# Attention stage: the value products of two units issued together every second unit, with three buffers of exponentials and two slots of part rows

## The reference

```python
# first attention: rotary embedding on q and k, no mask
att = softmax(einsum('bhqd,bhkd->bhqk', q, k) / sqrt(16));  y = att @ v;  x = x + y @ wo.T
# second attention: no rotary embedding, a linear bias by distance and a causal mask
att = softmax(q @ k / sqrt(16) + alibi + causal_mask);      y = att @ v;  x = x + y @ W_o
```

## Time and profile before

| what | value |
|---|---|
| median of three runs | 2952.81 us |
| the profiled execution's own time | 2950.72 us |
| its span in the trace | 2948.9 us |
| TensorE busy | 2667.6 us, 90% |
| VectorE busy | 1946.6 us, 66% |
| ScalarE busy | 1261.4 us, 43% |
| GpSimd busy | 657.1 us, 22% |
| granted TensorE clock, mean | 0.949 |

### The profile page before, as it was taken

How to read it: one execution, slowest core, us unless ns; L and a number is a source line. 1 busy time by engine, 2 the same in 40 slices (tenths; PEclk the granted TensorE clock), 3 DMA queues, 4 the chain that set the end, 5 groups by cost and what they waited for, 6 DMA issues and landing times. The chain is left out here.

```text
span 2948.9 us, 40309 instructions
## 1 busy us (share of the span) xinstructions
PE 2667.6 (90%) x14292; PEld 1275.0 (43%) x14292; DVE 1946.6 (66%) x4227; ACT 1261.4 (43%) x1901; POOL 657.1 (22%) x640
## 2 busy tenths in 40 slices
PE   3987999999999999797999995999999999798997
PEld 2442233333333332354455663454544454455564
DVE  5877878777877885585774334767677674576333
ACT  1432456556655667443211221355455556221221
POOL 0554122131230300153002441222121100001341
PEclk8996899999999999998999997799999999899998
DMA  3004330321303300001202663633233430301566
GB/s 118 1 1 101 49 60 12 54 50 22 60 17 49 58 8 1 1 1 61 92 33 49 137 135 85 129 64 57 45 61 54 66 50 2 107 33 33 122 138 166
DMA packets 163075, 175.78 MB, mean 60 GB/s; under 512 B 19570, under 2 KB 136242, under 8 KB 162738
## 3 DMA queue, kind: packets, MB, share of 16 engines
q1 hardware_dynamic: 145348, 150.48, 22.9%
q0 software_dynamic: 12416, 17.84, 3.8%
q10 hardware_dynamic: 5120, 4.98, 0.5%
HBM read 116.32 MB, written 56.13 MB: 58 GB/s over the span
## 5 line engine op out<-in xcount | busy, mean ns | idle before, releaser
L1776 DVE TENSOR_REDUCE a_mx<-a_bank 128x1 f32<-128x512 f32 (+3 forms) x1792 | 1031.0, 627 | 285.3 <-PE a_bank L1517 219.0
L1653 ACT ACTIVATE a_E<-a_bank 128x1024 f32<-128x1024 f32 (+3 forms) x896 | 794.8, 932 | 477.5 <-PE a_bank L1574 328.3
L1517 PE MATMUL a_bank<-a_KT,a_QT 96*128 96x512 bf16 (+4 forms) x1792 | 597.0, 379 | 35.1 <-DVE a_mx L1776 25.2
L1574 PE MATMUL a_bank<-a_QT,a_KT 99*128 99x512 bf16 (+4 forms) x1792 | 510.7, 360 | 18.5 <-DMA a_QT<-a_mT 16.0
L1589 PE MATMUL a_bank<-a_E,a_Vg 128*32 128x512 f32 (+3 forms) x3584 | 442.3, 566 | 0.7 <-ACT a_E L1653 0.7
L1517 PEld LDWEIGHTS a_bank<-a_KT,a_QT 96*128 96x128 bf16 (+1 forms) x1792 | 152.2, 98 | 526.1 <-DVE a_mx L1776 305.6
L1574 PEld LDWEIGHTS a_bank<-a_QT,a_KT 99*128 99x128 bf16 (+1 forms) x1792 | 170.4, 99 | 199.0 <-ACT a_E L1653 37.0
L848 PE MATMUL d_bank<-wdT,d_hT 128*128 128x256 f32 (+1 forms) x768 | 201.9, 407 | 21.7 <-DVE x L1054 21.7
L960 ACT ACTIVATE d_silu<-d_bank 128x512 f32<-128x512 f32 x96 | 57.2, 596 | 375.6 <-PE d_bank L835 368.4
L1044 DVE SCALAR_TENSOR_TENSOR d_silu<-d_silu,d_bank 128x512 f32<-128x512 f32 x96 | 65.6, 683 | 227.3 <-ACT d_silu L960 219.9
L433 POOL TENSOR_TENSOR f_hl<-f_hT,f_hh 128x512 f16<-128x512 f32 x96 | 111.1, 1157 | 392.1 <-ACT f_hh L452 392.1
(11 more groups left out here) (234 smaller groups left out, 3537.8 us busy)
## 6 DMA issues: line engine op xcount, KB each, us to landing
parts<-a_parts SPq DMA_DIRECT2D x64, 384.0 KB, 2.5
a_QT<-parts SPq DMA_DIRECT2D x180, 128.0 KB, 5.4
a_KT<-parts SPq DMA_DIRECT2D x180, 128.0 KB, 8.0
d_wgu<-in_L_ffn_w_gate SPq DMA_DIRECT2D x64, 176.0 KB
d_wgu<-in_L_ffn_w_up SPq DMA_DIRECT2D x64, 176.0 KB
d_wd<-in_L_ffn_w_down SPq DMA_DIRECT2D x64, 176.0 KB
normalised<-d_xn SPq DMA_DIRECT2D x8, 1152.0 KB, 4.7
acc<-d_zero SPq DMA_DIRECT2D x66, 128.0 KB, 1.8
```

The lines of the kernel that those rows point to most:

```text
L1517: last = nc.tensor.matmul(out[:, 0:w], QT[0:W, h, qt * P:(qt + 1) * P], KT[0:W, h, kh * HALF:kh * HALF + w], start=True, stop=not diag)
L1574: last = nc.tensor.matmul(out, KT[:, h, kt * P:(kt + 1) * P], QT[:, h, half * HALF + c0:(half + 1) * HALF], start=True, stop=not diag)
L1653: nc.scalar.activation(E[:, u % 2, 2 * pair:2 * pair + 2, c0:HALF], bank[:, 2 * pair:2 * pair + 2, c0:HALF], ACT.Exp).then_inc(exps, 1)
L1776: nc.vector.tensor_reduce(mx[:, j, qt, kh:kh + 1], out[:, 0:w], AX.X, ALU.max).then_inc(freed_dve, 1)
```

## The change

- The value products are issued in even units only: in an even unit `u` those of `u-2` and then `u-1`, in unit 0 the last two of the group before. Odd units have none. After the last group the last two are issued as before.
- `E` has three buffers, used by `(G * U + u) % 3`; the exponentials of a unit wait for the products of the unit three before it.
- `Ysb` has one slot in place of two; a second copy waits for the `turn_y` of the first.
- `parts` has two slots in place of four. At the first sequence rows 2 and 3 are held in the third buffer of `E`, and the exponentials of group 0, unit 2 wait for their writes. `split` now waits for the write of two before (four before in the first cases).

```diff
-        parts = sb(tag + "parts", [P, 4, 3, HALF], BF16)
+        parts = sb(tag + "parts", [P, 2, 3, HALF], BF16)
-        E = sb(tag + "E", [P, 2, GH, HALF])
-        Ysb = sb(tag + "Ysb", [P, 2, HALF])
+        E = sb(tag + "E", [P, 3, GH, HALF])
+        Ysb = sb(tag + "Ysb", [P, HALF])
...
+        def part_rows(b, n):
+
+            if b == 0 and n in (2, 3):
+                rows = E[:, 2].rearrange("p j c -> p (j c)").bitcast(BF16)
+                return rows[:, (n - 2) * 3 * HALF:(n - 1) * 3 * HALF].rearrange("p (s c) -> p s c", s=3)
+            return parts[:, n % 2]
...
-                    if b or n >= 4:
-                        pool.wait_ge(written[n % 4], START + (done // 4) * 16)
+                    user = done - 2 if done >= 6 else done - 4
+                    pool.wait_ge(written[user % 4], START + (user // 4 + 1) * 16)
...
-                        if u:
+                        if u % 2 == 0 and u:
+                            pv_unit(G, u - 2)
                             pv_unit(G, u - 1)
-                        elif G:
+                        elif u % 2 == 0 and G:
+                            pv_unit(G - 1, U - 2)
                             pv_unit(G - 1, U - 1)
                         for x in beside[G, u][2:]:
                             fill(x)
+                pv_unit(BG - 1, U - 2)
                 pv_unit(BG - 1, U - 1)
...
-                    if pair == 0 and (G or u > 1):
-                        act.wait_ge(pv, START + G * U + u - 1)
+                    if pair == 0 and G * U + u > 2:
+                        act.wait_ge(pv, START + G * U + u - 2)
+                    if G == 0 and u == 2 and pair == 0:
+                        for n in (2, 3):
+                            act.wait_ge(written[n], START + 16)
...
-                    if G:
-                        act.wait_ge(filled, START + place["turn_y", G - 1, half] + 1)
-                    nc.scalar.activation(Ysb[:, half, :], bank[:, 4, :], ACT.Copy).then_inc(y_kept, 1)
+                    if G or half:
+                        act.wait_ge(filled, START + place["turn_y", G if half else G - 1, 1 - half] + 1)
+                    nc.scalar.activation(Ysb[:], bank[:, 4, :], ACT.Copy).then_inc(y_kept, 1)
```

More of the change, by code:

```diff
@@ L1395, in write @@
                     dst = dram["parts"][b, 1 - c % 2, :, c // 2 * P:(c // 2 + 1) * P, half * HALF:(half + 1) * HALF]
-                    sp.dma_start(dst.rearrange("s p t -> p s t"), parts[:, n % 4]).then_inc(written[n % 4], 16)
+                    sp.dma_start(dst.rearrange("s p t -> p s t"), part_rows(b, n)).then_inc(written[n % 4], 16)
                 def load(b, g):
@@ L1447, in split @@
                     at_ = slice(half * HALF, (half + 1) * HALF)
-                    p = parts[:, n % 4]
+                    p = part_rows(b, n)
                     if second:
@@ L1527, in fill @@
                         for i in range(KPH):
-                            last = nc.tensor.transpose(out[:, i * P:(i + 1) * P], Ysb[:, x[2], i * P:(i + 1) * P], ident)
+                            last = nc.tensor.transpose(out[:, i * P:(i + 1) * P], Ysb[:, i * P:(i + 1) * P], ident)
                     elif kind == "tokens":
@@ L1589, in pv_unit @@
                         last = nc.tensor.matmul(bank[VW * j:VW * (j + 1), 4, c0:HALF], Vg[:, G % NG, kt, VS * j:VS * j + VW],
-                                                E[:, u % 2, j, c0:HALF], start=first, stop=final, tile_position=(0, VW * j))
+                                                E[:, (G * U + u) % 3, j, c0:HALF], start=first, stop=final, tile_position=(0, VW * j))
                     last.then_inc(pv, 1)
@@ L1652, in exp_pair @@
                     act.wait_ge(scored, START + G * 2 * U + 2 * u + pair + 1)
-                    nc.scalar.activation(E[:, u % 2, 2 * pair:2 * pair + 2, c0:HALF], bank[:, 2 * pair:2 * pair + 2, c0:HALF],
+                    nc.scalar.activation(E[:, (G * U + u) % 3, 2 * pair:2 * pair + 2, c0:HALF], bank[:, 2 * pair:2 * pair + 2, c0:HALF],
                                          ACT.Exp).then_inc(exps, 1)
@@ L1668, in cast @@
                         act.wait_ge(roped_dve, START + 2 * n + 2)
-                    nc.scalar.activation(parts[:, n, 0], staged(0, n)[0], ACT.Copy).then_inc(high, 1)
+                    nc.scalar.activation(part_rows(0, n)[:, 0], staged(0, n)[0], ACT.Copy).then_inc(high, 1)
                 def cast_rest(n):
                     act.wait_ge(rest, START + n + 1)
-                    nc.scalar.activation(parts[:, n, 1], staged(0, n)[0], ACT.Copy).then_inc(mid, 1)
+                    nc.scalar.activation(part_rows(0, n)[:, 1], staged(0, n)[0], ACT.Copy).then_inc(mid, 1)
                 for x in ahead_of_rows[0:8]:
@@ L1744, in middle @@
                     dve.wait_ge(high, START + n + 1)
-                    nc.vector.tensor_tensor(staged(0, n)[0], staged(0, n)[0], parts[:, n, 0], ALU.subtract).then_inc(rest, 1)
+                    nc.vector.tensor_tensor(staged(0, n)[0], staged(0, n)[0], part_rows(0, n)[:, 0], ALU.subtract).then_inc(rest, 1)
                 def lower(n):
                     dve.wait_ge(mid, START + n + 1)
-                    nc.vector.tensor_tensor(parts[:, n, 2], staged(0, n)[0], parts[:, n, 1], ALU.subtract).then_inc(parted_dve, 1)
+                    nc.vector.tensor_tensor(part_rows(0, n)[:, 2], staged(0, n)[0], part_rows(0, n)[:, 1], ALU.subtract).then_inc(parted_dve, 1)
                 def maxima(G):
```

## The result

The changed kernel takes 2983.56 us (median of four runs, 2978.78 to 2988.76) against 2954.39 before (median of four): ratio 1.0096, 95% interval 1.0069 to 1.0123. It is slower, as forecast; the forecast of 2990, 1.0126 of the 2952.81 it was worked out from, lies just above the interval and above all four runs. The profiled execution spans 2977.7 us, 28.8 more than before.

A forecast was written before the change was run, and what follows sets the result against it. TensorE ends last, with VectorE close behind at 89% in plain first-stage groups. 29 + 6 + 0 + 2 = +37 on 2950.7 gives 2988, and 2.1 for the runs' median 2990 us; 8 in 10 from 2944 to 3012.

The forecast's parts named there:

- The block: Two units' value products together take 2.21 us; on TensorE alone a two-unit cycle falls from 5.67 to 5.47.
- the switch isn't saved: Rival: the second unit's weight loads wait, block 2.42 us, 45 us more than forecast, 3035 us; chance 0.04.
- VectorE rushed, the wait at h: Plain first-stage cycle: TensorE waits 0.38 us for a bank at h, its last odd-unit chunk; cycle 5.89 against 5.67.
- TensorE's gain comes through: Rival: VectorE keeps ahead of the three banks, each cycle gains 0.20 us, -45 in all, 2908 us; chance 0.08.
- ScalarE "isn't late": First-stage cycle: the odd unit's exponentials are there at 3.1 us, when TensorE comes at 3.25.
- The first stage's 29 us in chunk cycles: First-stage cycles with chunks lose 4 + 23 + 2 = 29 us over the groups; bounds -24 and +42.
- stalls are taken in: Rival: long items, DMA waits and clock dips absorb stalls, only last groups lose; 2950 to 2965 us; chance 0.12.
- Cycles without chunks: Ten first-stage cycles: ScalarE runs out of scores during the block, 5.0 to 5.1 us each for 4.23; +6 us.
- The second stage at 0: Its 88 chunk cycles gain 0.20 us and lose 0.19 each; put at 0, between -18 and +19.
- Values after the wait for `m_rows`: `turn_m` stands ahead of one more unit's products, one more lies behind the wait; the sum is the same, costing nothing.
- Buffers and narrow slots at nothing: Third `E` buffer, single `Ysb` and two `parts` slots cost nothing; late writes at the second stage's start are hidden.
- the narrow slots reach the path: Rival: at the second stage's start the two `parts` slots cost 10 us more, 3000 us; chance 0.04.

The follow-up runs named there:

- e5: The changed kernel with first-stage maxima over half the columns and first-stage exponentials over half the queries (from the fourth unit on); 2895.71 us.
- e6: The kernel before the change with first-stage maxima over half the columns and first-stage exponentials over half the queries; 2902.14 us.
- e3: The changed kernel with first-stage maxima taken over the first half of each chunk's columns only; 2921.58 us.
- e1: The changed kernel's buffers with the value products issued in every unit again; 2952.21 us against 2952.28 before, ratio 1.0001.
- e7: The changed kernel, but with products single wherever the unit of the block holds no chunk; 2979.05 us, ratio 1.0093 to the kernel before.
- e12: The kernel before with turn_m and the maxima rows' DMAs one unit earlier, and products together in the second stage only; 2937.15 us, ratio 0.9953.
- e8: The changed kernel with products together only in second-stage units 0 and 6 of a group (not the last group), all others single; 2959.28 us, ratio 1.0026.
- e4: The kernel before the change with first-stage maxima over half of each chunk's columns; 2904.56 us.
- e9: The changed kernel with three of an even unit's items ahead of the block in place of two; 2966.64 us, ratio 1.0051 to the kernel before.

## Why the prediction was right

- **The block.** Forecast 2.21 us, measured 2.16, and the gain on TensorE alone 0.20 against the 0.24 that e5 and e6 show. The switch is saved, so the rival "the switch isn't saved" (2.42) is out. The third stream came at the lower bound (0.43), not at the row I took.
- **VectorE rushed, the wait at h.** Right in place and size: h came 0.38 late as forecast, the cycle took 5.85 for 5.89, and shorter maxima removed the wait (5.74). The rival "TensorE's gain comes through" needs VectorE and ScalarE both relieved; e5 is what it would look like.
- **ScalarE "isn't late".** Right for this kernel (3.1 against 3.25), and it hid that ScalarE is the next bound, 0.15 us behind. e3 shows it.
- **The first stage's 29 us in chunk cycles** was the term that came out smaller: the stage's 27.4 less 5.4 in the last group and 1.4 in the four chunkless units before it leave 21 (28 if e1's trace is taken for the order before, so the doubt of 7 us covers the miss). The plain group lost 1.9 (2.3 forecast: eight blocks 0.05 shorter). The groups with token items went from 69.5 and 71.1 to 69.7, where I had +1.4 each; that their long waits took the stalls in fits the rival "stalls are taken in", but these groups move by 1.6 us between two traces of one order. As a whole that rival (2950 to 2965 us) is out. The groups with projections in odd units lost 4.0 (52.1 to 56.1) where I had 2.1: a cycle with such an item takes 8.05 for 7.40, as that step of the walk has it, and I had averaged it away.
- **Cycles without chunks**: +6 forecast for the ten of the first stage, 6.8 traced (5.4 in the last group, 1.4 in the two before), at 5.09 us a cycle for 5.0 to 5.1, and all returned when those units are single (e7). The last group of the second stage: +2 forecast, 2.2 traced, 1.2 of it returned.
- **The second stage at 0** was right in sum, wrong in cause. I had the saved 0.20 and a lost 0.19 cancel in each cycle, and said of the waits for `m_rows` that the sum is the same. In fact the stage loses 6.0 us once those waits are gone (e12), 3.8 of it in the 88 chunk cycles that I had put at 0. The changed order took about 5 us out of the waits: in the second stage their PE row was 6.4 us before and is 1.5 after.

```profile
PE a_bank L1574 <- DMA a_QT<-a_mT: 6.4, 8, 2.1
```

```profile
PE a_bank L1581 <- DMA a_QT<-a_mT: 1.5, 1, 1.5
```

The 39.5 us in the prediction add the weight loads' row to the matmuls', which are the same waits seen twice; what TensorE lost there was 16.0 us in both stages. The step "Values after the wait for `m_rows`" failed: it counted units, but these are not equal. The unit that `turn_m` overtakes is 512 queries wide, the one that moves behind the wait 256. At the 0.43 us that a stream of 512 takes, two streams each, that is 0.43 us for each of 15 groups, 6 us. That is worked out, not run by itself; e8, where the cover shrinks by the same 256 queries, lost 1.7 us more in these waits.
- **Buffers and narrow slots at nothing**: e1 shows it, and the rival "the narrow slots reach the path" is out. The margin was thin, though. GpSimd waited 13.99 us for the write of row 4 at the start of the second stage:

```profile
1903.80 0.61 POOL L1467 CAST a_parts<-a_y 128x512 bf16<-128x512 f32 x1 [13.99 <-DMA parts<-a_parts]
```

and the four writes on SyncE, which took 2.30 us in the earlier trace rows, now end only 2.4 us before the rows are issued:

```profile
1895.78 16.43 SPq L1403 DMA_DIRECT2D parts<-a_parts  x4
1914.57 3.00 SPq L1422 DMA_DIRECT2D a_QT<-a_mT  x4
```

The rows are issued 5.6 us ahead of the first score (1920.2), as before (5.7), so it stayed hidden.

What stays open is the rest of e4's and e9's gains around the sequences' ends: the group lengths show where they lie, and no run takes those groups apart.

## What to carry to other kernels

Batching work on the busiest engine saves its switches, but it also bunches what the next engine must take: count how many of its items must pass between two batches through the buffers that there are, and compare that floor with the present cycle before counting the saving. When a change comes out even in one stage, look for two effects that cancel: in the second stage here the harmful one hid behind an unrelated wait that had become shorter, and moving the cause of that wait alone (the transposed maxima one unit earlier) was worth 0.7%.

## What the runs showed of the hardware

- Float32 products of 32 columns that follow one another without leaving the narrow tiles run at 0.43 us per stream of 512 columns, with the next weights loaded underneath (1108.28 in the changed kernel); going in and out once more costs 0.24 us, by the cycles of 5.67 (e6) and 5.43 (e5).
- A write of 384 KB that SyncE issued at 1895.78, behind 24 loads, had landed 8.0 us later, when the copy that waited for it began (1903.80); the median of such writes in this trace is 2.5 us.
- A stall shows as different lengths in the two rows of TensorE: 0.50 us in the weight loads' and 0.21 in the matmuls' for one of 0.38 (1106.20 in the changed kernel). Adding the two rows counts it twice.
- The granted clock was 1.00 in plain groups of both kernels and in the last group, though TensorE idled 6 of 31.2 us there in pieces of up to 0.74 us.
